# Routed experts of a transformer block: the tile loops written out, token rows buffered eight deep, and the combining pass moved into the same block

## What is computed

```
normed = h * rsqrt(mean(h^2) + 1e-8) * norm_weight          # T = 4096 tokens
shared = relu(normed @ sw1 + sb1) @ sw2 + sb2               # hidden width 512
scores, idx = top_k(sigmoid(normed @ router_w.T), 2)        # 2 of 8 experts
w      = scores / (sum(scores) + 1e-6)
routed = sum over the two chosen e of  w_e * (relu(normed @ ew1[e] + eb1[e]) @ ew2[e] + eb2[e])
out    = x + gb * (shared + routed)
```

## Time and profile before

| profiled execution | us |
|---|---|
| its own time | 858.44 |
| span, first to last instruction | 856.7 |
| median of the three timed runs | 858.69 |

### The profile page before, as it was taken

The page is one execution under the profiler, slowest core; times in us unless marked ns, Lnnn a source line. Parts: engine busy times, 40 slices in busy tenths (PEclk is TensorE's granted clock), DMA queues, the critical chain, the costliest instruction groups (busy, mean ns, idle before and its releaser), DMA issues. The chain is left out here.

```text
span 856.7 us, 15853 instructions
## 1 busy us (share of the span) xinstructions
PE 672.8 (79%) x5361; PEld 408.3 (48%) x5361; DVE 450.7 (53%) x1304; ACT 427.7 (50%) x749; POOL 306.0 (36%) x492
## 2 busy tenths in 40 slices
PE   4457899989898998989844588898665899999920
PEld 3223343333433343444312456666545788888820
DVE  1558787868587666767413345777541222222217
ACT  5120567665665666656731367677223445445500
POOL 2332323142433323313123227656730444444420
PEclk9999899999999999999975889999887999999975
DMA  8334232333332334311133601111124767767719
GB/s 157 108 106 153 83 105 89 119 114 115 119 108 100 116 100 141 111 66 56 52 105 121 161 28 54 44 51 42 58 79 137 202 194 207 200 199 202 204 36 280
DMA packets 98448, 101.07 MB, mean 118 GB/s; under 512 B 13152, under 2 KB 81672, under 8 KB 98288
## 3 DMA queue, kind: packets, MB, share of 16 engines
q1 hardware_dynamic: 89360, 87.45, 34.0%
q0 software_dynamic: 4544, 9.45, 3.1%
q10 hardware_dynamic: 4480, 3.35, 1.7%
HBM read 60.54 MB, written 37.57 MB: 115 GB/s over the span
## 5 line engine op out<-in xcount | busy, mean ns | idle before, releaser
L1043 DVE TENSOR_REDUCE row_max<-ps_s 128x1 f32<-128x384 f32 (+3 forms) x384 | 216.9, 595 | 94.4 <-PE ps_s L780 74.1
L626 ACT ACTIVATE work<-ps_s 128x1024 f32<-128x1024 f32 (+1 forms) x192 | 168.4, 884 | 66.7 <-PE ps_s L809 64.0
L780 PE MATMUL ps_s<-k_st,q_st 128*128 128x384 bf16 (+3 forms) x512 | 130.7, 312 | 0.0
L1569 POOL DMA_INDIRECT y_d<-res,target x78 | 74.8, 959 | 115.5 <-DVE res L1639 103.7
L777 PE MATMUL ps_s<-later_q,ident_b 128*128 128x128 bf16 (+1 forms) x384 | 94.8, 251 | 18.0 <-DVE row_max L1043 13.5
L826 PE MATMUL ps_pv<-work,v_sb 128*32 128x512 f32 (+3 forms) x1024 | 95.2, 445 | 1.3 <-ACT ctx_raw L660 1.2
L777 PEld LDWEIGHTS ps_s<-later_q,ident_b 128*128 128x128 bf16 x384 | 37.4, 98 | 116.6 <-DVE row_max L1043 81.7
L1635 DVE TENSOR_TENSOR biased<-ps_s,bias 128x256 f32<-128x256 f32 x39 | 16.6, 425 | 130.2 <-PE ps_s L1621 127.1
L1621 PEld LDWEIGHTS ps_s<-w_tile,x_hidden 128*128 128x128 f32 x624 | 75.6, 192 | 2.0
L1611 PE MATMUL ps_s<-tok_t,w_tile 128*128 128x256 f32 x312 | 76.1, 388 | 0.0
L1621 PE MATMUL ps_s<-w_tile,x_hidden 128*128 128x128 f32 x624 | 75.8, 275 | 0.0
(11 more groups left out here) (206 smaller groups left out, 1038.4 us busy)
## 6 DMA issues: line engine op xcount, KB each, us to landing
w_tile<-in_ew SPq DMA_DIRECT2D x39, 514.0 KB
ctx_d<-ctx_raw SPq DMA_DIRECT2D x32, 256.0 KB, 2.7
q_st<-q_d SPq DMA_DIRECT2D x64, 102.0 KB
k_st<-k_d SPq DMA_DIRECT2D x64, 96.0 KB
rows<-slots_d SPq DMA_DIRECT2D x39, 132.0 KB
got<-y_d SPq DMA_DIRECT2D x16, 256.0 KB, 5.3
q_d<-qk_part SPq DMA_DIRECT2D x8, 384.0 KB, 2.5
k_d<-qk_part SPq DMA_DIRECT2D x8, 384.0 KB, 2.7
```

Of the source, the lines that this page charges most:

```text
L626: act.activation(dst, src, ACT.Exp, scale=SCALE).then_inc(exp_done, 1)
L780: mm = pe.matmul(bnk[:, k * keys:(k + 1) * keys], q_st[b % 2][:, g, j, i * P:(i + 1) * P], k_st[b % 2][:, g, j // 2, 0:keys], start=False, ...
L1043: dve.reduce_max(row_max[:, m % 2, js[0] % 2, j:j + len(js), i], src, AXIS.X).then_inc(max_taken, 1)
L1569: pool.indirect_dma_start(y_d[:], bass.IndirectOffsetOnAxis(ap=target[:, k, c:c + 1], axis=0), res[:, k, c, :], None).then_inc(put[k], 16)
```

## The change

`attend()` and `dense()` are untouched. In `experts()`:

- The hardware loops are gone on all engines: Python writes out the 39 tiles, tile numbers are constants, and the waits are for constants.
- `rows` and its semaphores are eight deep (`DEEP`). SP issues rows 0, weights 0, rows 1 to 3, and then for t = 1, 2, ... rows t+3, weights t. Rows of tile t wait for `res_ready` of tile t-8, weights and bias of tile t for `bias_added` of tile t-4 (before: both for `res_ready` of tile t-4). The arithmetic on PE, ACT and DVE and its order are as before.
- POOL no longer waits for its scatters; SP waits for them and goes on to the loads of the combining pass.
- `combine()` is gone as a block. Its loads follow on SP, its passes on DVE and its stores on ACT in the block of the experts. `got` holds all eight batches, `routed` is gone (the passes are in place), and a batch's loads wait only for those of batch b-4 to land, as they share a semaphore. For batches 2 and 5 POOL does the sum of the two choices.

The core of the diff; what is left out are allocations, and the same replacement of loop body by Python loop on ACT, PE and DVE:

```diff
-            HALVES, BUF = SLOTS // P, 4
+            HALVES, BUF, DEEP = SLOTS // P, 4, 8
...
+                rows = sb("rows", [P, DEEP, HALVES, ROW], until=own)
+                got = sb("got", [P, B, 2, NT, D], until=own)
...
+                BY_POOL = (2, 5)
+                MIX_STEPS = [sum(2 if k in BY_POOL else 3 for k in range(b)) for b in range(B + 1)]
...
-                        def body(st):
-                            t, k = st.t, st.buffer(0, BUF)
-
-                            wait_apart(sp, res_ready, HALVES * (t - BUF + 1), v_zeroed)
-                            row = sp.value_load(tile_row[0:1, bass.ds(t, 1)], min_val=0, max_val=N_REGION * E + SPARE_ROWS // SLOTS - 1)
+                        def load_rows(t):
+
+                            k = t % DEEP
+                            wait(sp, res_ready, HALVES * (t - DEEP + 1))
+                            row = sp.value_load(tile_row[0:1, t:t + 1], min_val=0, max_val=N_REGION * E + SPARE_ROWS // SLOTS - 1)
...
-                            e = sp.value_load(tile_expert[0:1, bass.ds(t, 1)], min_val=0, max_val=E - 1)
+
+                        def load_weights(t):
+
+                            k = t % BUF
+                            wait(sp, bias_added, t - BUF + 1)
+                            e = sp.value_load(tile_expert[0:1, t:t + 1], min_val=0, max_val=E - 1)
...
-                        tiles(sp, body)
+
+                        load_rows(0)
+                        load_weights(0)
+                        for t in range(1, BUF):
+                            load_rows(t)
+                        for t in range(1, N_TILES):
+                            if t + BUF - 1 < N_TILES:
+                                load_rows(t + BUF - 1)
+                            load_weights(t)
+                        for k in range(BUF):
+                            sp.wait_ge(put[k], 16 * HALVES * len(range(k, N_TILES, BUF)))
+                        for b in range(B):
+                            wait(sp, got_in[b % 4], 32 * (b // 4))
+                            for c in range(2):
+                                sp.dma_start(got[:, b, c], y_r[:, c, NT * b:NT * (b + 1), :]).then_inc(got_in[b % 4], 16)
...
-                        tiles(pool, body)
-                        for k in range(BUF):
-                            pool.wait_ge(put[k], 16 * HALVES * len(range(k, N_TILES, BUF)))
+                        for b in BY_POOL:
+                            pool.wait_ge(got_in[b % 4], 32 * (b // 4 + 1))
+                            pool.tensor_tensor(got[:, b, 0], got[:, b, 0], got[:, b, 1], ALU.add).then_inc(pool_mixed, 1)
...
-                                pe.wait_ge(rows_in[k], loads(t, k))
-                                wait(pe, tok_out, t - 1)
+                                pe.wait_ge(rows_in[k], 16 * ((t + 1) // DEEP + 1))
+                                wait(pe, tok_out, t)
...
+                            if b in BY_POOL:
+                                dve.wait_ge(pool_mixed, BY_POOL.index(b) + 1)
+                            else:
+                                dve.wait_ge(got_in[b % 4], 32 * (b // 4 + 1))
+                                dve.tensor_tensor(got[:, b, 0], got[:, b, 0], got[:, b, 1], ALU.add).then_inc(mixed, 1)
+                                done += 1
+                                dve.wait_ge(mixed, done)
+                            dve.tensor_tensor(got[:, b, 0], got[:, b, 0], gate_b[:, b:b + 1, :].to_broadcast([P, NT, D]), ALU.mult).then_inc(mixed, 1)
+                            dve.wait_ge(mixed, done + 1)
+                            dve.tensor_tensor(got[:, b, 0], got[:, b, 0], h_sb[:, NT * b:NT * (b + 1), :], ALU.add).then_inc(mixed, 1)
...
-        combine()
```

More of the change, by code:

```diff
@@ L1526, in experts @@
                 target = sb("target", [P, BUF, HALVES], U32, until=own)
-                rows_in = [sem(f"rows_in{k}") for k in range(BUF)]
+                got = sb("got", [P, B, 2, NT, D], until=own)
+                rows_in = [sem(f"rows_in{k}") for k in range(DEEP)]
                 w_in = [sem(f"w_in{k}") for k in range(BUF)]
@@ L1531, in experts, with tok_bank, real @@
                 l2_done, res_ready, bias_added = sem("x_l2_done"), sem("res_ready"), sem("bias_added")
+                got_in = [sem(f"got_in{k}") for k in range(4)]
+                mixed, pool_mixed, stored = sem("mixed"), sem("pool_mixed"), sem("stored")
                 slots_r = slots_d.rearrange("(t c p) w -> p t c w", p=P, c=HALVES)
[L1534 to L1545, removed]
+                y_r = y_d[0:2 * B * S, :].rearrange("(c n p) d -> p c n d", p=P, c=2)
+                BY_POOL = (2, 5)
+                MIX_STEPS = [sum(2 if k in BY_POOL else 3 for k in range(b)) for b in range(B + 1)]
+                def tok_bank(t):
+                    return (ps_m, ps_pv)[t % 2]
+                def real(t):
+                    return 0 <= t < N_TILES
                 with nc.Block() as block:
@@ L1560, in body @@
                                 .then_inc(w_in[k], 16)
-                        tiles(sp, body)
+                        load_rows(0)
[12 more added lines that the diff above has]
+                                sp.dma_start(got[:, b, c], y_r[:, c, NT * b:NT * (b + 1), :]).then_inc(got_in[b % 4], 16)
                     @block.gpsimd
                     def _(pool):
-                        def body(st):
-                            t, k = st.t, st.buffer(0, BUF)
-                            wait_apart(pool, res_ready, HALVES * (t + 1), v_zeroed)
+                        for t in range(N_TILES):
+                            k = t % BUF
+                            pool.wait_ge(res_ready, HALVES * (t + 1))
                             for c in range(HALVES):
@@ L1570, in body @@
                                     ap=target[:, k, c:c + 1], axis=0), res[:, k, c, :], None).then_inc(put[k], 16)
-                        tiles(pool, body)
-                        for k in range(BUF):
-                            pool.wait_ge(put[k], 16 * HALVES * len(range(k, N_TILES, BUF)))
+                        for b in BY_POOL:
+                            pool.wait_ge(got_in[b % 4], 32 * (b // 4 + 1))
+                            pool.tensor_tensor(got[:, b, 0], got[:, b, 0], got[:, b, 1], ALU.add).then_inc(pool_mixed, 1)
                     @block.scalar
                     def _(act):
[L1577 to L1582, removed]
+                        for t in range(-1, N_TILES):
+                            if real(t + 1):
+                                act.wait_ge(turned, t + 2)
+                                wait(act, l1_done, NF // 2 * (t + 1 - BUF + 1))
+                                act.activation(tok_t[:, (t + 1) % BUF], tok_bank(t + 1)[:, 0:SLOTS], ACT.Copy, scale=col("norm_w"))\
                                     .then_inc(tok_out, 1)
-                            if st.has(0):
-                                t, k = st.t, st.buffer(0, BUF)
+                            if real(t):
+                                k = t % BUF
                                 for f in range(NF):
@@ L1614, in body @@
                                         mm.then_inc(l1_done, 1)
[L1615 to L1618, removed]
+                            if real(t - 1):
+                                k = (t - 1) % BUF
+                                pe.wait_ge(relu_done, NF * t)
+                                wait(pe, bias_added, t - 2)
                                 for c in range(HALVES):
@@ L1623, in body @@
                                 mm.then_inc(l2_done, 1)
-                        x_steps(pe, body)
                     @block.vector
                     def _(dve):
[L1628 to L1632, removed]
+                        for t in range(N_TILES):
+                            k, r = t % BUF, t % DEEP
+                            wait(dve, put[k], 16 * HALVES * (t // BUF))
+                            dve.wait_ge(rows_in[r], 16 * (t // DEEP + 1))
+                            dve.tensor_copy(target[:, k], rows[:, r, :, D:D + 1].rearrange("p c a -> p (c a)").bitcast(U32))
                             dve.wait_ge(l2_done, t + 1)
@@ L1638, in body @@
                             for c in range(HALVES):
[L1639 to L1655, removed]
-                        for b in range(B):
[L1657 to L1679, removed]
```

22 lines of the change are left out of this document (13 added, 9 removed).

## The result

The changed kernel takes 835.86 us (median of four runs, 833.97 to 836.68); the kernel before, in runs beside it, 858.9. The ratio is 0.9733, 95% interval 0.9711 to 0.9755, so it saves some 23 us.

What follows compares the result with a forecast made beforehand. PE was taken to set the pace in the experts, with 11.8 us of waits for rows; -11.8 + 1.9 - 6.7 + 0.3 = -16.3 us from 858.44 gives 842.1, stated as 842.3, range 838.0 to 849.0.

Steps and rivals of the forecast that it cites:

- The step: Experts, PE: with rows issued earlier the waits for rows go and a step takes 3.93 us; -11.8 us.
- the best case: Experts, PE: the step comes down to 3.89 us, which bounds the gain at -13.3 us.
- The start: Start of the experts: weights 1 go out three turns later, delaying layer 1 of tile 1; +1.9 us, bounds 0 and +3.5.
- The seam: Between experts and combining: SP's first load no longer comes behind POOL's drain at the block end; -6.7 us.
- Rival A: Between experts and combining: whatever POOL waits for in its drain might hold back SP's loads; 849.0 us, chance 0.07.
- The passes: Combining: DVE loses two sums and a store's wait, but POOL's sums hold it up; +0.3 us, bounds -1.8 and +1.2.
- the sign: Combining: if the forecast is right, DVE passes of over 1.2 us appear beside each POOL sum.
- B: Experts: weights take the place of rows, the step stays near 4.25; 854.1 us, half of it 848.2; chance 0.09.
- C: Experts: written-out code must be fetched, stopping PE; 866 us, chance of slower 0.03; milder form 851.5, chance 0.05.

Runs made afterwards that it cites:

- the seam alone: Kernel before, its loops and four-deep rows kept, with SP waiting for the scatters and the combining in the same block; 850.58 us, ratio 0.9915.
- the shallow kernel: Changed kernel with four buffers of rows and SP issuing rows and weights of a tile together as before, still written out; 848.52 us, ratio 0.9873.
- the old order: Changed kernel with SP loading rows and weights of tiles 0 to 3 in turn at the start, as before; 825.83 us, ratio 0.9760.

## Why the prediction fell short

**The step (term -11.8, measured -18.4).** The step of the reasoning that failed is "PE's own step is about 3.95 us", and the sentence "less 11.8 that is 141.4, or 3.93 a step, which agrees with the 3.95 above". I took the time between two transposes, less the recorded idle, for PE's own work. PE's own step is 3.73. The agreement of the two figures was no check, since both leave out the same delay: what PE loses behind the modelled end of a matmul is not recorded as idle. From 665.83 on the kernel before has no step of 3.73 at all; 33 steps (to 806.12) were 17.2 us longer than that in sum, and the waits recorded in them are 10.6 of the 11.8. Of the rest, 4.3 us lie in front of the transposes too, without a record, and 2.3 behind them, where late transposes and the layer 1 after them take some hundredths more. Three of the experiments settle it: deep rows in a hardware loop give 3.73, deep rows with PE looped give 3.73, written-out code with shallow rows gives 4.235.

The figure was to be had beforehand, from a place in the timeline of the kernel before where nothing was late:

```profile
740.76 1.95 PE L1621 MATMUL ps_s<-w_tile,x_hidden 128*128 128x128 f32 x16
742.55 0.39 PE L1603 MATMUL ps_m<-ident,rows 128*128 128x128 f32 x2
742.77 1.89 PE L1611 MATMUL ps_s<-tok_t,w_tile 128*128 128x256 f32 x8
744.50 1.95 PE L1621 MATMUL ps_s<-w_tile,x_hidden 128*128 128x128 f32 x16
```

From layer 2 to the next transposes 1.79, to layer 1 0.22, to layer 2 1.73: 3.74. The 3.89 that I gave as the best case has no row behind it: whole steps of the kernel before go down to 3.79, and even these have a delay somewhere.

What set the old step was a ring over two of them: transposes, layers, bias sum, scaling, SP's read and issue, the rows' landing, and again transposes. To the earlier trace rows belongs the start of that ring:

```profile
730.07 0.44 PE L1603 MATMUL ps_pv<-ident,rows 128*128 128x128 f32 x2 [0.68 <-DMA rows<-slots_d]
```

From there to the bias sum of that step's layer 2 are 4.43 us (734.50), to SP's issue 1.83 (736.33), to the transposes of those rows 2.32 (738.65): 8.58 in all, for two steps. Over 36 steps two took 8.51 in the kernel before, 8.45 with the seam alone and 8.47 in the shallow kernel, in which no engine had a loop and SP's counts were constants.

**The start (+1.9, measured +2.6).** The mechanism was right: weights 1 go out at 655.43 and layer 1 of tile 1 starts at 660.27, 4.8 after it and not 4.5. It now waits 1.9 us for them. Of its shift by 2.5 us against the kernel before 1.9 go away with the old order (10.0 to 8.2 us behind the first transposes); the other 0.6 is there with the old order too, and my term had nothing for it: rows of tile 1 are transposed 3.57 us behind those of tile 0 instead of 3.21, and PE is at the low clock for longer.

**The seam (-6.7, measured -7.4).** Right, and shown by undoing it and by doing it alone. Of the further 0.7, 0.5 is in the written-out code ahead of the load: from bias sum 36 to the end of POOL's last scatter it takes 9.48 instead of 9.96. In the kernel with the seam alone, still looped, it is 9.96. Rival A (the drain's cause holds the loads) is refuted.

**The passes (+0.3, measured +0.8).** Kernels with POOL's sums have passes of 17.50 to 18.24 us, so the +0.8 of one execution decides nothing on the size. The +0.3 holds another 0.3 for a store that no row of mine shows; the trace of the kernel before has that wait of DVE. Right in kind: DVE's pass of 1.63 beside POOL's is longer than the 1.2 that I gave as the sign, and POOL's is lengthened too. The rule of the Trainium skill that I cited beside it (*SBUF — State Buffer*, "Who interferes with whom") would have put this at +1.1; the trace lies between. I had both of POOL's sums hold a pass of DVE, and only the second did; the first shows another form of the price: DVE was not held, it waited 1.15 us for POOL's result.

**Rivals B and C.** Weights did not take the place of rows: DMA went from share 0.70 to 0.82, and one step in 33 waited 0.4 us for weights. The written-out stream had seven fetches in the 125 us in which PE was busy for 124.86 and every other step took 3.73 or 3.74, so they cost nothing. The queue's row for this stretch:

```profile
q8 instruction: 7, 0.11, 0.4%
```

**The range.** Its lower end took a step of 3.89 as the best case. With every recorded wait gone, the right floor is the one that PE's instructions give back to back: 36 steps of 3.73 are 134.3 us, a bound of -18.9 where I had -13.3.

## What to carry to other kernels

Take an engine's own step from the starts of its instructions in a step in which nothing is late, part by part, never from a period less its recorded waits: in TensorE's records here delays up to the 0.16 us of modelled tail leave no idle time behind, and each recorded one is longer than its record by as much. When a load is released by the result of work a few tiles back, find the ring that it closes; here deeper buffers with earlier issue broke it, and writing the loops out did not. In this kernel a block's end behind POOL's indirect DMAs cost every engine POOL's drain of 6.4 us: put what follows into the same block, and let the drain run beside it.

## What I had not expected of the hardware

POOL's DRAIN in a block with indirect DMAs took 6.4 to 6.5 us, counted from the end of POOL's last operation or wait: 6.4 behind a wait for the scatters, 6.4 behind the last scatter itself, 6.5 behind a sum that ended 17 us after it. In a block with the same sums and no indirect DMA it ended 0.1 us behind the last sum. So the long drain comes with the block that holds the scatters; what POOL does in these 6.4 us no run shows. A hardware loop on PE with register arithmetic ahead of its waits cost nothing measurable: 134.34 us for 36 steps, looped or written out.
